# Splitting the next tokens behind a block's last inner chunk, and adding a block's residual at the start of the next block

## The reference, cut to what matters

```python
gate_logits = h2 @ Wg
w, sel = jax.lax.top_k(gate_logits, 1)
hid = jax.nn.relu(jnp.einsum('nd,edf->enf', h2, W1) + b1[:, None, :])
y = jnp.einsum('enf,efd->end', hid, W2) + b2[:, None, :]
moe = jnp.einsum('ne,end->nd', combine, y)
return x + moe.reshape(b, t, d)
```

## Time and profile before

| what | value |
|---|---|
| median of 3 runs | 1289.19 us (1286.11 to 1289.38) |
| the profiled execution | 1285.7 us, its span 1284.0 us |
| mean granted TensorE clock | 0.925 |
| expert part (first weight matmul to the end) | 778 to 1284 us |
| a block without conversions | 50 us |
| blocks 4, 5, 6 (one block to an expert) | 57.2, 58.8, 57.2 us |

### The profile page before, as it was taken

How to read it: one execution, slowest core, us unless ns; L and a number is a source line. 1 busy time by engine, 2 the same in 40 slices (tenths; PEclk the granted TensorE clock), 3 DMA queues, 4 the chain that set the end, 5 groups by cost and what they waited for, 6 DMA issues and landing times.

```text
span 1284.0 us, 19500 instructions
## 1 busy us (share of the span) xinstructions
PE 1074.4 (84%) x6126; PEld 685.3 (53%) x6127; DVE 804.6 (63%) x1503; ACT 557.2 (43%) x740; POOL 340.0 (26%) x175
## 2 busy tenths in 40 slices
PE   0459877899969958999999605989998989898997
PEld 0335546754755745558887502545555545454554
DVE  1366767876462874428876517896224998889732
ACT  0336755630331114417762207774113676677611
POOL 3000000037000340207000145563001655656400
PEclk9979998999979978997999657999999999899999
DMA  8720020002330440011000099997002999999600
GB/s 319 293 89 0 0 76 24 1 1 99 96 50 1 113 84 13 1 44 48 2 2 1 8 222 339 343 343 269 21 25 64 352 321 354 327 351 341 226 25 27
DMA packets 98242, 170.50 MB, mean 133 GB/s; under 512 B 38395, under 2 KB 38667, under 8 KB 98194
## 3 DMA queue, kind: packets, MB, share of 16 engines
q1 hardware_dynamic: 88002, 145.20, 33.3%
q0 software_dynamic: 6016, 16.80, 4.1%
q10 hardware_dynamic: 4176, 7.87, 1.9%
HBM read 153.05 MB, written 18.79 MB: 134 GB/s over the span
## 4 chain that ended last, share of the span: by engine, by line
PE 63%; DVE 13%; issue 9%; DMA 5%; SPq 3%; ACT 3%; POOL 3%; DVEq 2%; POOLq 0%; ACTq 0%
PE psum L1316 30%; PE psum L1526 13%; PE psum L1505 12%; PE psum L1305 3%; DMA area<-in_L_gnn_a_dst_dram 2%; PE psum L1354 2%; POOL area L628 1%; DMA sorted_tokens<-area,smalls 1%; PE psum L1514 1%; SPq L441 1%; SPq L439 1%; DMA low<-in_L_ffn_W_dram 1%; DVE low L1275 1%; DVE smalls L911 1%; DVE low L1017 1%
## 5 line engine op out<-in xcount | busy, mean ns | idle before, releaser
L1316 PE MATMUL psum<-area,low 128*125 128x256 f16 (+2 forms) x1080 | 248.5, 392 | 21.2 <-DVE low L1096 10.9
L1526 PE MATMUL psum<-area,low 128*128 128x384 f16 x1296 | 232.3, 339 | 27.0 <-DVE low L1282 16.7
L628 POOL TENSOR_TENSOR area<-low,area 128x1536 f16<-128x1536 f32 x48 | 189.2, 3944 | 179.0 <-ACT area L841 178.7
L1505 PE MATMUL psum<-area,low 128*128 128x512 f16 x972 | 220.7, 383 | 9.5 <-DVE area L1248 9.5
L1316 PEld LDWEIGHTS psum<-area,low 128*125 128x125 f16 (+1 forms) x1080 | 150.5, 150 | 114.2 <-issue 63.1
L841 ACT ACTIVATE area<-low 128x1536 f16<-128x1536 f32 x144 | 203.3, 1470 | 8.5 <-DMA low<-in_L_ffn_W_dram 6.9
L1248 DVE TENSOR_TENSOR area<-low,area 128x1536 f16<-128x1536 f32 x96 | 198.2, 2107 | 10.8 <-ACT area L841 10.8
L1526 PEld LDWEIGHTS psum<-area,low 128*128 128x128 f16 x1296 | 130.3, 101 | 117.1 <-issue 44.8
L1316 PE MATMUL psum<-area 125*125 125x64 f16 (+9 forms) x1076 | 163.7, 305 | 12.1 <-DVE area L1234 8.0
L1505 PEld LDWEIGHTS psum<-area,low 128*128 128x128 f16 x972 | 95.9, 99 | 121.2 <-issue 14.7
L1316 PEld LDWEIGHTS psum<-area 125*125 125x125 f16 (+2 forms) x1076 | 118.9, 161 | 41.7 <-issue 14.1
(11 more groups left out here) (198 smaller groups left out, 1206.7 us busy)
## 6 DMA issues: line engine op xcount, KB each, us to landing
low<-in_L_ffn_W_dram SPq DMA_DIRECT2D x144, 768.0 KB, 6.6
area<-in_L_gnn_W_dram SPq DMA_DIRECT2D x2, 3072.0 KB, 26.5
area<-in_L_gnn_Wr_dram SPq DMA_DIRECT2D x2, 3072.0 KB, 31.0
sorted_tokens<-area POOLq DMA_DIRECT2D x3, 1792.0 KB, 20.4
sorted_totals<-area POOLq DMA_DIRECT2D x3, 1792.0 KB, 41.9
low<-sorted_tokens ACTq DMA_DIRECT2D x11, 384.0 KB, 5.7
low<-in_x_dram SPq DMA_DIRECT2D x10, 375.0 KB
low<-sorted_totals ACTq DMA_DIRECT2D x9, 384.0 KB, 2.9
```

The costliest lines, as they stand in the source:

```text
L628: pool.tensor_tensor(low_, raw_view(u), high_, ALU.subtract).then_inc(pool_low_ok, 1)
L1316: ins = pe.matmul(place(name)[0:parts, at:at + w], left(q), right(q)[:, at:at + w], start=(q == 0), stop=(q == k - 1))
L1505: ins = pe.matmul(psum[:, (c % 2) * BANK:(c % 2 + 1) * BANK], ht[x_][:, k, :], w1_s[c][w_][:, k, :], start=(k == 0 and x_ + w_ == 0), stop ...
L1526: ins = pe.matmul(psum[:, (4 + q) * BANK:(4 + q) * BANK + D // 2], hidT[c % 2][x_][:, j, :], w2_s[c][w_][:, j, q * D // 2:(q + 1) * D // 2 ...
```

## The change

Four edits. First, on VectorE `tokens_low` goes behind low(5), and on ScalarE `tokens_high` goes behind the high half of chunk 5. Second, the load of the tokens after next is issued in step 7, ahead of the conversion of u6 to u8, instead of behind it. Third, the add leaves the end of a block and becomes `add_rest(b)` at step 1 of the next block, behind the conversion of u9 and u10 and ahead of relu(0); one more stands behind the loop. Fourth, since the first block now adds too, PSUM banks 4 and 5 are cleared once on VectorE, and GpSimd's clearing of `y_o` raises `rest_in`.

```diff
-        def expert_blocks(eng, convert, first_tokens, block_steps, block_end):
+        def expert_blocks(eng, convert, first_tokens, block_steps):
...
-                block_end(b)
...
-            link(pool.memset(y_o, 0.0))
+            pool.memset(y_o, 0.0).then_inc(rest_in, 32)
...
-                if s_ == C:
-                    tokens_high(b + 1)
                 if 1 <= s_ <= C:
                     c = s_ - 1
                     act.wait_ge(relu_ok, b * C + (c + 1))
                     act.wait_ge(hid_used, b * C + (C + c - 1))
                     act.activation(hidT[c % 2][0], v3(relu, CK), ACT.Copy).then_inc(hidhi_ok, 1)
-
-            def block_end(b):
-
-                act.wait_ge(ht_ok, b + 2)
-                act.dma_start(xt, hs_dram[bass.ds(b * BR + 2 * BR, BR), :]).then_inc(xt_in, 16)
+                if s_ == C:
+                    tokens_high(b + 1)
+                if s_ == C + 1:
+                    act.wait_ge(ht_ok, b + 2)
+                    act.dma_start(xt, hs_dram[bass.ds(b * BR + 2 * BR, BR), :]).then_inc(xt_in, 16)
...
+                if s_ == 1:
+                    add_rest(b)
                 if 1 <= s_ <= C:
...
-                    if c == C - 1:
-                        tokens_low(b + 1)
                     dve.wait_ge(hidhi_ok, b * C + (c + 2))
                     dve.tensor_tensor(hidT[c % 2][1], v3(relu, CK), hidT[c % 2][0],
                                       ALU.subtract).then_inc(hid_relu, 1)
-
-            def block_end(b):
-
-                dve.wait_ge(hid_used, b * C + 2 * C)
+                    if c == C - 1:
+                        tokens_low(b + 1)
+
+            def add_rest(b):
+
+                dve.wait_ge(hid_used, b * C + C)
                 dve.wait_ge(rest_in, b * 32 + 32)
...
-            dve.sem_inc(y_cp, 1)
-            expert_blocks(dve, low_part, first_tokens, block_steps, block_end)
+            was_emptied(dve, ("b2sum", T - 1))
+            dve.memset(psum[:, 4 * BANK:6 * BANK], 0.0)
+            expert_blocks(dve, low_part, first_tokens, block_steps)
+            blocks = dve.value_load(nblocks[0:1, 0:1], min_val=1, max_val=NB)
+            add_rest(blocks)
```

More of the change, by code:

```diff
@@ L880, in first_tokens @@
                 act.dma_start(xt, hs_dram[BR:2 * BR, :]).then_inc(xt_in, 16)
-            expert_blocks(act, high_part, first_tokens, block_steps, block_end)
+            expert_blocks(act, high_part, first_tokens, block_steps)
             blocks = act.value_load(nblocks[0:1, 0:1], min_val=1, max_val=NB)
```

## The result

| | before | after |
|---|---|---|
| median of 4 runs each | 1287.65 us (1284.84 to 1289.38) | 1314.51 us (1313.32 to 1315.57) |
| ratio, with its 95% interval | | 1.0207 (1.0187 to 1.0228) |
| profiled execution, its span | 1285.7 us, 1284.0 us | 1315.57 us, 1313.7 us |
| mean granted TensorE clock | 0.925 | 0.921 |

The changed kernel is 26.9 us slower. The forecast was 1309 us with a range of 1284 to 1318.

The account below looks back on a forecast made before the run. VectorE's chain, not TensorE, was taken to set the boundary of blocks with conversions. Lateness in six blocks, less idle time and with block 0's add, came to 23.6 us on the profiled 1285.7: 1309 us, range 1284 to 1318.

Parts of the forecast that it names:

- The resource and the boundary: From block end to the next low(0), VectorE's gapless chain sets the end; TensorE's 0.9 us gain at chunk 5 is waited away.
- The step that decided, u11 behind `y_cp`: On GpSimd, `send_rows` and u11 wait for the moved add, which ends at 853.76 instead of 850.43; u11 ends 859.3.
- The turns at the port: Late u11 holds u12, and u14 goes ahead of u13, 2.96 us a hold; VectorE is 4.7 us late at u15.
- signs named for *right: Among them: u12 and u13 at 3.9 to 4.7 us each, low(0) at 0.69, chunk 1 stalls of about 2 us.
- What that did to TensorE: low(0) 1.0 us earlier, with chunk 0's second product; stalls of about 2 us ahead of the second product of chunk 1.
- The sum by block: VectorE's lateness in blocks 0, 1, 4, 5, 6 and 7, less idle time, plus block 0's 0.95 us add: 23.6 us.
- near 62: A sign of being right: blocks 4 and 6 would take near 62 us each.
- the 2.04 us of the earlier trace: Idle time in blocks 5 and 7, 0.68 + 1.36 us in block 5, taken off the 4.7 us lateness.
- The split "for nothing": Token split behind chunk 5: TensorE starts 0.9 us earlier five times, waited away at the next wait; VectorE's chain gains nothing.
- Half the price: Rival: u14 comes behind u13 each time, u15 starts 2.2 us late instead of 4.7; 1295 us, chance 0.17.
- Nothing: Rival: VectorE's lateness stays under TensorE's room, decided at about 2 us; 1286 to 1291 us, chance 0.12.
- faster: Rival: GpSimd's turns cost no more; low(0) 1.0 us earlier, TensorE gains 4.4 + 8; 1279.7 or 1273 us, chance 0.16.

Follow-up runs that it names:

- split_only: The kernel before with only the token split moved behind chunk 5 on both engines; 1295.94 us against 1290.86, ratio 1.0038.
- before_delay6: The kernel before with six small clearings of unused columns on GpSimd between `send_rows` and u11 in first blocks; 1313.33 us against 1290.86, ratio 1.0188.
- add_only: The changed kernel with the token split put back ahead of chunk 5, the other three edits kept; 1315.62 us against 1290.86, ratio 1.0197.
- before_delay3: The kernel before with three small clearings on GpSimd ahead of u11; 1303.11 us against 1289.00, ratio 1.0109.
- after_u11_first: The changed kernel with GpSimd doing u11 ahead of its wait for `y_cp` and of `send_rows`; 1294.36 us against 1290.86, ratio 1.0033.
- before_u11_first: The kernel before with GpSimd doing u11 ahead of its wait for the add and of `send_rows`; 1295.78 us against 1289.00, ratio 1.0041.
- split_few: The kernel before with u5 and u8 given to VectorE and the token split moved behind chunk 5; 1282.23 us against 1289.00, ratio 0.9939.

## Why the prediction was right, and where it wasn't

**The resource and the boundary: right.** That VectorE's unbroken chain sets the start of a first block, and that TensorE's gain at chunk 5 is waited away, is shown by `split_only` (no gain; its 5.2 us at chunk 5 show in no block) and by `before_delay6` (a delay on GpSimd alone, which touches neither the add nor the split, costs 1.9%).

**The step that decided, u11 behind `y_cp`: right.** Taking u11 from behind that wait alone takes 1.0207 to 1.0033.

**The turns at the port: right in number, one of them on another instruction.** The forecast took 1.63 us for `send_rows` from the earlier trace rows, so it had u11 start at 856.3, when low(0) was over, and hold u12. `send_rows` took 1.01 us, so u11 came 2.0 us behind relu(0)'s start, 0.13 us behind low(0)'s, and low(0) ended only behind it. Forecast 4.7 late at u15 (4.9 by relu(1)), measured 5.0 by relu(1). u14 ahead of u13 came as forecast, six times of six, each time 4.64 or 4.65 us for u13; the wait for DMA of the earlier trace rows did not come back in block 4. So two of the signs named for *right* failed, and a third follows below: low(0) took 3.77 to 3.82 us, not 0.69, and u12 kept its 1.75.

**What that did to TensorE: wrong place.** I had low(0) 1.0 us early and a stall of about 2 us ahead of the second product of chunk 1. Instead the stall is ahead of that of chunk 0 (5.18 us in block 1), and its product runs 5.4 to 7.0 us. The second product of chunk 1 then starts 15.9 to 17.5 us behind relu(0), before 12.6 to 14.2, because TensorE's own queue is late, not because low(1) is. VectorE was late by nearly the same 5 us either way.

**The sum by block.** In the order of blocks 0, 1, 4, 5, 6 and 7:

| | 0 | 1 | 4 | 5 | 6 | 7 | sum |
|---|---|---|---|---|---|---|---|
| forecast | 5.65 | 3.95 | 4.7 | 2.7 | 4.7 | 1.9 | 23.6 |
| measured | 0.9 + 4.5 | 4.2 | 4.4 | 3.3 | 4.6 | 2.7 | 24.6 |

Blocks 4 and 6 are at 61.7 and 61.8 us against "near 62". But the sum hands on VectorE's lateness in every block, and in three of the six it isn't what counts. In block 5 the second product of chunk 1 starts 17.52 us behind relu(0) (at 1087.12), before 14.24 (relu(0) at 1068.05). The first row is from the changed kernel, the second from the kernel before:

```profile
1104.64 4.06 PE L1529 MATMUL psum<-area,low 128*128 128x384 f16 x24
1082.29 4.06 PE L1526 MATMUL psum<-area,low 128*128 128x384 f16 x24
```

That is 3.3 us later, and in blocks 6 and 7 it is 4.6 and 2.7: in these three the block's whole loss, to 0.02 us. There the loss is TensorE's, its wait and its slow product at chunk 0. In blocks 0, 1 and 4 TensorE is 4.0, 3.8 and 3.4 us later there, less than the loss, which fits VectorE's 5.0 less some room. That the sum comes so near in blocks 5 to 7 is partly luck.

In blocks 5 and 7 less idle time took it off than the 2.04 us of the earlier trace rows: I had counted it as room for VectorE. It was there because TensorE was late: in the execution shown, the second product of chunk 0 took 5.7 us in just these two blocks. After the change it takes 7.0 and 6.4, so TensorE is later again; the equality above bears this out, but no run tries it. The forecast lies 5.5 us under the median after. About 2 of these lie between the profiled execution and the median of before (1285.7 and 1287.65 by all four runs), 1.0 in the sum; the rest is less than the spread of single executions.

**The split "for nothing": under-sized.** It was priced at 0 with the 0.9 us "waited away". By itself it costs 0.38% (0.18 to 0.59); in the execution shown that is 3.9 us of longer products at chunk 0, less the 0.5 us won in block 0. In the changed kernel, where the wait there is 3.5 us or more with the split and without, `add_only` and the changed kernel don't differ (1.0197 and 1.0207).

**The rivals.** *Half the price* is real (`before_delay3`, two blocks), but there u14 came 1.66 and 1.97 us behind the start of u12, in the changed kernel 0.4 to 0.9. *Nothing* and *faster* fall: the lateness was 5 us, not under 2. Of the 8 us for full clock behind low(5) some came: the product of chunk 5 took 25.0 us in five blocks instead of 30.5. But that of chunk 0 took 37.0 us in six instead of 27.7. The time that *faster* gave for all its gains together was mis-added: 1285.7 less 6.0, 4.4 and 8 is 1267.3, and 1273 leaves out the 6.0.

The Trainium skill's rule that a VectorE instruction with two SBUF inputs and GpSimd's exclude each other for the whole instruction (SBUF — State Buffer, "Who interferes with whom") is borne out by the 3.80 us of low(0) beside u11; relu and the add, which read PSUM, kept 1.10 to 1.13 and 0.94 to 0.96 us everywhere, the add also in `after_u11_first`, where it lies beside u11.

## What to carry to other kernels

Before an instruction with a semaphore is moved, list what stands behind the waits for that semaphore on every other queue: the moved instruction costs its 0.9 us, its followers may cost five. Where two engines exclude each other, put the second engine's work on stretches in which the first does what doesn't collide (here relu out of PSUM), and see whether less of it is better: two pieces fewer on GpSimd made this kernel 0.7% faster; a third fewer brought no more (0.9953 against 0.9933). A wait that looks like pure loss may be what keeps a piece of work in such a stretch.

## What the runs showed of the hardware

- A turn at the shared port is worth 2.9 us. Where VectorE had two conversions in a row, GpSimd won the turn between them when its piece was recorded as started up to 1.61 us behind the start of the first (1.30 to 1.61 in the six such starts of `before_delay3` and `before_u11_first`), and lost it at 1.66 and 1.97. A high half that came 0.25 us late for its DMA went with a start of a block of 8.1 instead of 11.0 us.
- The recorded starts don't always give the order: in the changed kernel low(0) is recorded as started 0.10 to 0.17 us ahead of u11 in all six blocks, and was held for the whole of u11 all the same.
- GpSimd's clearing, which only writes, did not hold a VectorE subtraction (0.69 us beside it).
- The issue of the indirect DMA on GpSimd (`send_rows`) isn't of one length: mostly 1.63 to 1.65 us beside VectorE's conversions, 0.97 to 1.02 us where VectorE did relu or nothing, 1.25 to 1.28 where it began beside low(0), 2.33 us in the row above, where it was issued as u10 had just got the port, and 3.31 us in block 7 of `split_few`.
- GpSimd's recorded duration of a piece depends on what it meets: 3.09 to 3.12 us where VectorE stood still behind it, 4.71 where it had to wait for its turn. VectorE's held instruction ends 0.5 us (512 columns) or 1.6 us (1536) behind it.
